# Reordering a binarised 3x3 convolution over 16 image pairs, with the small threshold arithmetic and the filter arithmetic recast

## The reference

```
out = x + sum over n of beta[n] * (conv(An, W_eff) + sum(alpha) * bias[n])
```

## Time and profile before

| | |
|---|---|
| median of three runs | 203.67 us |
| the profiled execution | 203.54 us, of which the span in the trace is 201.8 us |
| granted TensorE clock, mean | 0.948 of full |
| TensorE busy | 169.1 us, 84% of the span |
| VectorE busy | 171.9 us, 85% |
| ScalarE busy | 140.7 us, 70% |
| GpSimd busy | 62.9 us, 31% |
| DMA queue of SyncE | 39.27 MB, 69.5% of the 16 engines' span |

### The profile page before, as it was taken

The page is one execution under the profiler, slowest core; times in us unless marked ns, Lnnn a source line. Parts: engine busy times, 40 slices in busy tenths (PEclk is TensorE's granted clock), DMA queues, the critical chain, the costliest instruction groups (busy, mean ns, idle before and its releaser), DMA issues.

```text
span 201.8 us, 4766 instructions
## 1 busy us (share of the span) xinstructions
PE 169.1 (84%) x1800; PEld 131.4 (65%) x1800; DVE 171.9 (85%) x422; ACT 140.7 (70%) x183; POOL 62.9 (31%) x76
## 2 busy tenths in 40 slices
PE   1484176499999899999898999999999998989871
PEld 0383074286868587868686877776868685757560
DVE  4369999998999999999999899999999999785132
ACT  2628466297979687979787889797979796853110
POOL 6175143433233314142315051414141414240000
PEclk9996559969999999999999999999999999999996
DMA  4799433062696889888788798889898565766525
GB/s 114 226 259 265 126 82 82 0 168 59 177 248 184 234 281 234 252 227 272 211 275 242 222 237 253 240 250 246 250 241 253 142 190 140 196 196 173 179 68 159
DMA packets 21030, 39.61 MB, mean 196 GB/s; under 512 B 9744, under 2 KB 9744, under 8 KB 21008
## 3 DMA queue, kind: packets, MB, share of 16 engines
q1 hardware_dynamic: 20272, 39.27, 69.5%
q10 hardware_dynamic: 736, 0.04, 0.2%
HBM read 13.15 MB, written 12.85 MB: 129 GB/s over the span
## 4 chain that ended last, share of the span: by engine, by line
PE 54%; DVE 16%; DMA 10%; ACT 6%; issue 5%; SPq 4%; POOL 2%; ACTq 0%; DVEq 0%
PE conv_ps L727 31%; PE y_ps L747 11%; PE x_ps L689 7%; DMA s_odd<-s_even 6%; ACT signs L348 5%; DMA params<-in_L_conv_beta 4%; DVE y_nat L550 3%; PE conv_ps L735 2%; PE conv_ps L730 2%; DVE raw_stats L559 2%; DVE s_even L621 2%; SPq L206 2%; DVE s_even L616 2%; SPq L207 1%; PE x_ps L697 1%
## 5 line engine op out<-in xcount | busy, mean ns | idle before, releaser
L727 PE MATMUL conv_ps<-s_even,w_mm 128*64 128x448 f16 (+1 forms) x576 | 105.0, 336 | 6.9 <-issue 2.8
L730 PE MATMUL conv_ps<-s_odd,w_mm 128*64 128x448 f16 (+2 forms) x576 | 105.2, 324 | 0.0
L348 ACT ACTIVATE signs<-x_ch,neg_thr 128x784 f16<-128x784 f32 x96 | 83.7, 938 | 0.8 <-DVE neg_thr L595 0.8
L727 PEld LDWEIGHTS conv_ps<-s_even,w_mm 128*64 128x64 f16 x576 | 60.8, 111 | 33.4 <-issue 11.5
L730 PEld LDWEIGHTS conv_ps<-s_odd,w_mm 128*64 128x64 f16 x576 | 60.8, 111 | 0.1
L550 DVE SCALAR_TENSOR_TENSOR y_nat<-y_ps,y_const,x_nat 112x1024 f32<-112x1024 f32 (+1 forms) x32 | 36.7, 1146 | 11.9 <-PE y_ps L747 11.7
L306 POOL TENSOR_SCALAR lo_part<-signs,ratio_lo 128x1568 f16<-128x1568 f16 x16 | 25.6, 1597 | 63.1 <-ACT signs L348 63.0
L689 PE MATMUL x_ps<-ident,x_nat 112*128 112x112 f32 x224 | 31.0, 285 | 13.8 <-ACT x_ch L343 11.4
L310 POOL TENSOR_SCALAR lo_part<-signs,ratio_lo 128x1568 f16<-128x1568 f16 x16 | 26.7, 1666 | 40.5 <-DVE half_hi L609 22.7
L361 ACT ACTIVATE y_ch<-conv_ps,y_scale 128x896 f32<-128x896 f32 (+1 forms) x32 | 28.9, 904 | 14.8 <-PE conv_ps L730 9.7
L689 PEld LDWEIGHTS x_ps<-ident,x_nat 112*128 112x128 f32 x224 | 26.3, 157 | 15.3 <-issue 13.6
(11 more groups left out here) (106 smaller groups left out, 93.3 us busy)
## 6 DMA issues: line engine op xcount, KB each, us to landing
x_nat<-in_x SPq DMA_DIRECT2D x16, 448.0 KB, 5.5
out<-y_nat SPq DMA_DIRECT2D x16, 448.0 KB, 4.3
s_odd<-s_even SPq DMA_DIRECT2D x32, 203.0 KB, 3.1
s_odd<-s_even SPq DMA_DIRECT2D x32, 188.5 KB, 3.0
x_nat<-in_x SPq DMA_DIRECT2D x16, 336.0 KB, 4.9
out<-y_nat SPq DMA_DIRECT2D x16, 322.0 KB, 2.7
s_odd<-s_even SPq DMA_DIRECT2D x32, 14.5 KB, 2.8
x_nat<-in_x SPq DMA_DIRECT2D x16, 14.0 KB, 5.7
```

Source lines behind the costliest of these rows:

```text
L348: act.activation(signs[q % 2][:, n, :, a, :], x_ch[q % CH_SLOTS][:, :, a, :], ACT.Sign, bias=neg_thr[q % 2][:, n, a:a + 1]).then_inc(signe ...
L727: last = nc.tensor.matmul(low[:, 0:n * ROWS], wt, s_even[b][:, part, r0:r0 + 2 * n, t:t + H], start=first, stop=end)
L730: last = nc.tensor.matmul(high[:, 0:m * ROWS], wt, s_odd[b][:, part, r0:r0 + 2 * m, t:t + H], start=first, stop=end and not at_edge)
```

## The change

The steps start at p = -1 and everything earlier is written out. The number of x buffers goes from 6 to 7 and that of `x_ch` from 3 to 4.

GpSimd's two scalings of a pair both wait for `half_made` and for the low sum of the pair before; those of pair 0 go to VectorE. In VectorE's step, pair_moments(r) goes between the two high scalings, the thresholds behind add_x(p, 0), the statistics of t behind them, and then come sum_high(q), sum_low(q) and add_x(p, 1). The thresholds' divisions and additions are now tensor_scalar instructions with one input from SBUF and per-partition scalars, one for each image, and the six thresholds are two instructions of three elements instead of three of two.

TensorE's step convolves bank 0 of half B, gathers the statistics of r, convolves bank 1, brings out, brings in the second half of t, convolves half A of p + 1, brings out, and brings in the first half of t + 1. The gather also waits until `x_ps` has been copied. ScalarE's step follows that order: root, scale_out, copy_in, sign image 0 of q, sign image 1 of r, scale_out, copy_in, sign image 2 of r.

Ahead of the steps the first halves of x are brought into other PSUM tiles, so that fewer wait for a copy. The parameters are loaded to one partition and spread by a product of TensorE. The five sign filters are weighted by ScalarE (`weigh_filter`) and added up by five products of TensorE into PSUM; VectorE makes `w_mm` out of PSUM (`split_filters`), and the filter's sizes are in `filter_sizes`. The order of products, stores, shifts and loads is otherwise as before.

```diff
-LEAD = 4
-X_SLOTS, CH_SLOTS, S_SLOTS = 6, 3, 3
+X_SLOTS, CH_SLOTS, S_SLOTS = 7, 4, 3
...
             def weigh_low(q):
-                pool.wait_ge(signed, 6 * q + 2)
-                if q:
-                    pool.wait_ge(lo_made, q)
+                pool.wait_ge(half_made, q + 1)
+                pool.wait_ge(lo_made, q)
                 ts(lo_part[0][:], signs[q % 2][:, 1].rearrange("p i a h -> p (i a h)"), ratio_lo[:, 0:1], 1.0,
                    ALU.mult, ALU.mult).then_inc(lo_weighed, 1)
-                pool.wait_ge(signed, 6 * q + 4)
-                pool.wait_ge(half_made, q + 1)
...
-            act.dma_start(params[:, 1, :], v.partition_broadcast(128)).then_inc(params_loaded, 16)
-            act.dma_start(params[:, 0, :], beta.partition_broadcast(128)).then_inc(params_loaded, 16)
-            act.dma_start(params[:, 2, :], bias.partition_broadcast(128)).then_inc(bias_loaded, 16)
-
-            def copy_in(q, f):
+            for i, t in enumerate((beta, v, bias)):
+                act.dma_start(params_row[:, i, :], t.unsqueeze(0)).then_inc(params_loaded, 16)
...
             def begin_signs(q):
-                act.wait_ge(thr_ready, 3 * (q + 1))
+                act.wait_ge(thr_ready, 2 * (q + 1))
                 if real(q - 2):
                     act.wait_ge(hi_made, q - 1)
-                    act.wait_ge(lo_weighed, 2 * (q - 1))
+                    act.wait_ge(lo_made, q - 1)
                 sign(q, 1)
...
+            def weigh_filter(m):
+                act.activation(w_parts[:, m, :].rearrange("p (a o c) -> p a o c", a=TAPS, o=2), filt[:, :, :, :, m],
+                               ACT.Copy, scale=neg_row[:, m, M_FIL:M_FIL + 1]).then_inc(w_weighed, 1)
+
             def step(p):
-                if real(p + 2):
-                    sign(p + 2, 2)
+                q, r, t = p + 2, p + 3, p + 4
+                if real(r):
+                    take_root(r)
                 if real(p):
                     scale_out(p, 1)
-                if real(p + 2):
-                    sign(p + 2, 0)
-                if real(p + 3):
-                    take_root(p + 3)
-                if real(p + LEAD):
-                    copy_in(p + LEAD, 0)
+                if real(t):
+                    copy_in(t, 1, y_ps if t == 3 else x_ps)
+                if real(q):
+                    sign(q, 0)
+                if real(r):
+                    begin_signs(r)
                 if p == -1:
-                    copy_in(p + LEAD, 1)
-                    begin_signs(p + 3)
                     act.wait_ge(y_scale_ready, 1)
                 if real(p + 1):
                     scale_out(p + 1, 0)
-                if p != -1:
-                    if real(p + LEAD):
-                        copy_in(p + LEAD, 1)
-                    if real(p + 3):
-                        begin_signs(p + 3)
+                if real(t + 1):
+                    copy_in(t + 1, 0)
+                if real(r):
+                    sign(r, 2)
...
+            act.wait_ge(solved, 1)
+            act.wait_ge(corners_zero, 2)
+            for m in range(M_FIL):
+                weigh_filter(m)
+            copy_in(2, 0)
+            copy_in(2, 1, y_ps)
+            take_root(1)
+            begin_signs(1)
+            copy_in(3, 0)
+            sign(1, 2)
+            for p in range(-1, PAIRS):
...
+                return [mark(ts(twice_dev[:, a:a + 1], moments[q % 2][:, a, 1:2], GN_EPS, inv_root[:, a:a + 1],
+                                ALU.add, ALU.mult)) for a in range(2)]
 
             def add_root(n):
-                settle(n)
-                return mark(tt(twice_dev[:], twice_dev[:], root[:], ALU.add))
+                for a in range(2):
+                    settle(n[a])
+                    n[a] = mark(ts(twice_dev[:, a:a + 1], twice_dev[:, a:a + 1], root[:, a:a + 1], None, ALU.add))
+                return n
 
             def make_thresholds(q, n):
-                settle(n)
-                for m in range(N_ACT):
-                    stt(neg_thr[q % 2][:, m, :], twice_dev[:], order[:, 1, m:m + 1], moments[q % 2][:, :, 0],
-                        ALU.mult, ALU.subtract).then_inc(thr_ready, 1)
-
-            def thresholds(q):
-                make_thresholds(q, add_root(divide_variance(q, invert_root(q))))
-
-            def weigh_high(q):
+                for a in range(2):
+                    settle(n[a])
+                    ts(neg_thr[q % 2][:, :, a], order[:, 1, :], twice_dev[:, a:a + 1], moments[q % 2][:, a, 0:1],
+                       ALU.mult, ALU.subtract).then_inc(thr_ready, 1)
+
+            def weigh_first(q):
...
+            def weigh_low(q, n):
+                mark(ts(lo_part[n - 1][:], flat(q, n), ratio_lo[:, n - 1:n], None, ALU.mult))
+
             def sum_low(q):
-                dve.wait_ge(lo_weighed, 2 * (q + 1))
+                if q:
+                    dve.wait_ge(lo_weighed, 2 * q)
+                else:
+                    settle()
...
                 if real(q):
-                    weigh_high(q)
+                    weigh_first(q)
+                if real(r):
+                    pair_moments(r)
+                if real(q):
+                    weigh_second(q)
                     sum_half(q)
                 if real(p):
                     add_x(p, 0)
                 if real(r):
-                    pair_moments(r)
-                if real(q):
-                    sum_high(q)
-                if real(r):
                     make_thresholds(r, add_root(divide_variance(r, invert_root(r))))
-                if real(p):
-                    add_x(p, 1)
-                if real(q):
-                    sum_low(q)
-                if p == -2:
-                    filter_parts()
                 if real(t):
                     lane_moments(t, 0)
                     lane_moments(t, 1)
                     spread_lanes(t)
+                if real(q):
+                    sum_high(q)
+                    sum_low(q)
+                if real(p):
+                    add_x(p, 1)
...
+            dve.wait_ge(gram_summed, 1)
+            link(nc.vector.tensor_copy(gram[:], solve_ps.rearrange("p (m n) -> p m n", m=M_FIL)))
+            k = pivot(0)
+            n = invert_root(0)
+            k = reduce(0, k)
+            n = divide_variance(0, n)
+            settle(k)
+            k = pivot(1)
+            n = add_root(n)
+            k = reduce(1, k)
+            dve.wait_ge(order_ready, 3)
+            make_thresholds(0, n)
...
+            substitute(1).then_inc(solved, 1)
+            dve.wait_ge(ratios_ready, 3)
+            weigh_first(0)
+            weigh_low(0, 1)
             lane_moments(1, 0)
-            eliminate(2)
+            weigh_second(0)
+            weigh_low(0, 2)
+            sum_half(0)
+            dve.wait_ge(pads_ready, 2 * S_SLOTS)
+            sum_high(0)
+            sum_low(0)
             lane_moments(1, 1)
             spread_lanes(1)
-            eliminate(3)
-            eliminate(4)
-            substitute()
-            dve.wait_ge(ratios_ready, 3)
-            dve.wait_ge(pads_ready, 2 * S_SLOTS)
-            for p in range(-2, PAIRS):
+            k = filter_sizes()
+            pair_moments(1)
+            split_filters(k)
+            make_thresholds(1, add_root(divide_variance(1, invert_root(1))))
+            lane_moments(2, 0)
+            lane_moments(2, 1)
+            spread_lanes(2)
+            output_const()
+            for p in range(-1, PAIRS):
...
             def step(p):
+                r, t = p + 3, p + 4
                 if real(p):
-                    convolve(p, 1)
+                    convolve(p, 1, (0,))
+                    if real(r):
+                        gather_lanes(r)
+                    convolve(p, 1, (1,))
                     bring_out(p, 0)
-                if p == -1:
-                    pe.wait_ge(hi_made, 1)
-                    for _ in range(WARM):
-                        nc.tensor.matmul(y_ps[:, 1, 0:128], ones[:], ones[:], start=True, stop=True)
-                if real(p + LEAD):
-                    bring_in(p + LEAD, 0)
-                if real(p + 3) and p != -1:
-                    gather_lanes(p + 3)
+                if real(t):
+                    if t > 3:
+                        pe.wait_ge(moments_ready, 2 * (r + 1))
+                        bring_in(t, 1)
+                    else:
+                        bring_in(t, 1, y_ps, 6)
                 if real(p + 1):
                     convolve(p + 1, 0)
                 if p == -1:
                     gather_lanes(2)
                 if real(p):
                     bring_out(p, 1)
-                if real(p + LEAD):
-                    bring_in(p + LEAD, 1)
+                if real(t + 1):
+                    if p == -1:
+                        pe.wait_ge(moments_ready, 6)
+                    bring_in(t + 1, 0)
...
+            bring_in(1, 0, conv_ps[1], 0)
+            bring_in(1, 1, y_ps, 2)
+            pe.wait_ge(moments_ready, 2)
```

(14 more changed lines are left out.)

141 lines of the change are left out of this document (78 added, 63 removed).

## The result

The changed kernel takes **211.56 us** (median of 4 runs, 210.76 to 212.46) against 202.72 for the kernel before on the same chip (4 runs): ratio 1.043, 95% interval 1.033 to 1.054. The forecast was 197.0 and the range ended at 209; the mechanism is that of rival A (209.0), with something on top. The profiled execution took 210.76 us, span 209.0, against a span of 201.8 before.

The account below looks back on a forecast made before the run. VectorE bounded the steps at 9.92 us, TensorE right behind at 9.64 and bounding afterwards. Eleven steps -4.0, beginning -1.9, end -0.6: -6.5 us from 203.54 gives 197.0; own range 194 to 201, 8-in-10 range 194 to 209.

Parts of the forecast that it names:

- rival A: VectorE's three-element thresholds wait for GpSimd's second scaling: 1.39 us a step, steps of 10.77, total 209.0 us; chance 0.32.
- 0.20 us less, if nothing holds them up.: VectorE's thresholds: 0.86 us against 1.06 a step, the two three-element instructions following at 0.07 and 0.13.
- S: End of the half sum, where both GpSimd scalings start; 119.77 in the earlier trace's step, scalings ending at S + 3.36.
- The high sum, -0.34: VectorE's high sum comes at about S + 4.4, finds GpSimd done: 0.34 us less a step, 0.92 instead of 1.26.
- The gather inside half B costs nothing by itself.: TensorE's step keeps the same instructions and stays at 9.64 us with the gather between the banks of half B.
- Stalls, 1.5 kept of 2.4: Stalls from shifts into `s_odd`, steps 1 to 12: 1.5 of 2.4 us kept, bounds 0 and 4.
- Rival B: New chain as long as the old step: late signs, less time for the high shift; about 202 us; chance 0.15.
- The beginning, -1.9: Up to step 1: first sign about 15.6, first convolution about 31.8; 1.9 us gained, bounds 1 lost and 3.5 gained.
- The end, -0.6: Last steps, nothing to bring in, run at TensorE's pace a little sooner: 0.6 us less, 0 to -1.5.
- The rule that was weighed: Skill's rule: one-input SBUF instructions take both ports when counts are even, or odd, over one and equal; cited for rival A.

Follow-up runs that it names:

- e7: Kernel before with one part of the change alone: both GpSimd scalings released by the half sum; 217.55 us, ratio 1.075.
- e4: Changed kernel with thresholds as six one-element instructions, plus a three-element scratch instruction behind them, its result unused; 213.08 us, ratio 1.053.
- e3: Changed kernel with the old threshold arithmetic (two inputs, two elements) in the new place; 217.59 us, ratio 1.076.
- e2: Changed kernel, three-element thresholds kept, GpSimd's second scaling also waiting for the next pair's thresholds; 205.88 us, ratio 1.021.
- e8: e2 with the high sum ahead of the lane statistics and GpSimd's second scaling waiting for that sum instead of the thresholds; 202.63 us, ratio 1.000.
- e12: e10 with a second matmul of the gathering's size between the banks of half A; 205.14 us, ratio 1.013.
- e10: e8 with, in step 0 alone, the gathering behind both banks of half B; 201.69 us, ratio 0.991.
- e11: e8, gathering behind both banks of B in every step, moments behind VectorE's second scaling, ScalarE's half scaling ahead of the root; 199.49 us, ratio 0.987.
- e9: e2 with, in step 0 alone, the gathering behind both banks of half B; 203.73 us, ratio 1.004.

## Why the prediction was wrong, by its own steps

**"0.20 us less, if nothing holds them up."** This is the step that failed. Something does: the first three-element threshold stands for GpSimd's second scaling. The prediction placed the boundary between the scalings at S + 1.74 to S + 1.79 and the threshold at S + 1.77, and chose that it slips between. Measured with S = 110.08 + 0.98 = 111.06: the second scaling starts at S + 1.64 and the threshold at S + 1.88. I was off by 0.15 on GpSimd (it starts S + 0.10, and the second starts 0.03 ahead of the first one's shown end instead of 0.05 behind) and by 0.11 on VectorE (the way from the reciprocal to the first threshold is 0.77, 112.17 to 112.94, and not 0.66: the two more tiny instructions were not free). A difference of 0.02 us had been read out of numbers that are good to 0.1. What decides, in all rows here, is whether VectorE's instruction already waits when a scaling ends: then it gets in (the high sum in step 13 at 186.77 and in e7, as the five-element instruction in the earlier trace rows); coming 0.05 (e4), 0.07 (e3) or 0.24 us later it stands for the whole of the next. It was not a coin toss of 53 to 32: a three-element instruction in the middle of 3.1 us of unbroken GpSimd work has to be costed as blocked.

And the block is not shorter even where it is free: from the reciprocal to the statistics 1.15 us (e2: 108.78 to 109.93) against 1.06 before. I took 0.07 and 0.13 for the two thresholds from instructions of another form that follow each other; what the trace shows for this form is 0.39 for both, and 0.26 for two one-element instructions. No run shows three-element ones at 0.07. Of the 0.29 us, 0.19 are these two and 0.10 the longer way to them. So +0.09 instead of -0.20.

**The high sum, -0.34.** Right in kind: it finds GpSimd done. It takes 0.98 and not 0.92: -0.28.

**Rival A's 10.77.** The trace shows 10.78, but by two errors that cancel: the base is 9.7 and not 9.38 (0.29 in the thresholds, 0.06 in the sum), the wait is 1.06 and not 1.39. Its 11 steps were 118.5, measured 119.73, the rest being stalls. Its end gave 2.0 back; in fact the end lost 0.5. The thresholds wait once more there (178.05, 1.54 us), and the low sum waits 1.47 us at 189.62 for the scaling of 187.30 (2.29 us); that these are the loss is not shown, since e8 has two such waits of 1.70 us and an end of 32.3.

**"The gather inside half B costs nothing by itself."** Wrong, by 0.30 us a step. Between two runs of products it costs 0.45 (e12 directly; half B takes 2.76 us in the trace of before, 51.64 to 54.40, and 3.21 in e10, 99.62 to 102.83). Behind eight transposes, where it was before, it cost 0.15 (1.01 us from their start to half A, 45.69 to 46.70, against 0.86 without it in e10, 98.76 to 99.62). TensorE's step is 9.94, not 9.64, exactly VectorE's old step of 9.92: the 0.28 us of VectorE that the forecast wanted to free was already spent on TensorE. This alone is 3.3 us in 11 steps.

**Stalls, 1.5 kept of 2.4.** Rival B's reason was right in part: the high sum starts at S + 1.3 in the earlier trace rows and S + 4.7 in e2, and its shift had less time. The statistics in front of it are 2.4 us of that. e8 against e2 puts 1.06 us in 11 steps on it in the traces.

Together, against the 107.5 us forecast for the 11 steps: 107.5 + 7.4 (the wait, changed kernel against e2) + 3.3 (the gathering) + 1.1 (the high sum) = 119.3; measured 119.73. But two of the three parts are differences between rows of the table, so all that this sum tests is 107.5 + 3.3 = 110.8 against the 111.23 of e8, and one trace of each kernel stands behind it. Only e2, e8 and e12 are direct; that all three could be had back at once is not shown: e11 got 110.17.

**The beginning, -1.9.** Measured -1.5, and the parts differ more than the sum. The first sign was at 15.29 (15.6 forecast). The first convolution came at 28.98, not 31.8: the warm-up shows 1.07 us on a clock that is already up, where the earlier trace rows has 1.94, and the bringing in lies under the filters' split. Then 2.2 of the 3.7 are gone again at step 1, by the gathering between the banks and, hidden behind it, the wait for the late high shift: e9 moves the first alone and gets 0.5 back. The wait at the gathering was in no step of the prediction, though both the instruction and what it waits for were in the diff. In e10 and e11, with both moved, step 1 is at 53.5, 4.3 us ahead of before.

**The end, -0.6.** Measured +0.5, as above.

**The rule that was weighed.** The one-element instructions ran free beside GpSimd (202 to 215 ns over all 32 of L602), the three-element ones did not (275 to 1362 ns over the 32 of L614). That is what the Trainium skill, page "Advanced Engine Details and Errata", section "2x-2p Requirements", says of counts that are equal and odd, over one. The trace agrees. I had given A a third of the chance, where that rule and the row with five elements both pointed the same way.

## What to carry to other kernels

Before GpSimd's work is made one unbroken stretch, list every VectorE instruction within SBUF that falls into it and count each as blocked to the end of the GpSimd instruction running then, unless a row shows its form running free there (here the one-element ones, and the statistics of e2 at 109.93, 1.97 us beside the scaling of 110.11); gaps of a few hundredths of a microsecond are no plan. A cheap cure is to let GpSimd wait, if it has slack: one wait moved to the idle engine was worth 4.4 to 7.4 us here. What a small instruction costs is best taken from rows of the same form: two of three elements took 0.39 us where 0.20 had been put down. And a matmul put between two runs of convolution products has a price three times that behind transposes: where TensorE's step is this close to the bound (9.64 against 9.92 us), cost it.

## What the runs showed of the hardware

- Who goes first where VectorE and GpSimd hold each other up: an instruction of VectorE that already waits when a GpSimd instruction ends goes ahead of GpSimd's next one, even where GpSimd's two are queued back to back (e7 at 105.97; the changed kernel's step 13 at 186.77), and that next one shows 2.29 instead of 1.57 us. One that comes 0.05 to 0.07 us behind GpSimd's start waits it out (e4, 39.99 against 39.94; e3, 105.47 against 105.40).
- A one-element VectorE instruction with per-partition scalars takes 0.20 to 0.21 us alone, and six in a row start 0.18 apart (1.09 us in all); two of three elements take 0.39. Six small ones are dearer than two wider ones by 0.70.
- A matmul of 128x24 in fp32 (x2 in the rows, 0.40 us) between convolution products costs 0.45 us of the path; behind transposes 0.15, ahead of transposes 0.24.
- 3.64 us of idle TensorE in step 0 were followed by half the clock, for 6 us in the changed kernel (40.4 to 46.5) and for 3 us in e2 (41.1 to 44.5); 2.31 us in the same place (e9) were not. In the kernel before, TensorE was idle for 3.01 us there, started again at 39.69 at full clock, and had half the clock from about 41.0 to 44.4.
